# Reciprocal norms moved from GpSimd's power to ScalarE's logarithm and exponential with a Newton step on VectorE

## The reference

```python
def l2norm(t):
    return t / jnp.maximum(jnp.linalg.norm(t, axis=-1, keepdims=True), 1e-12)

def attn_layer(x, Wqkv, qs, ksc, Wo):       # HEADS = 16, DIM_HEAD = 64, windows of 32
    q, k, v = jnp.split(x @ Wqkv, 3, -1)    # then split into heads
    q = l2norm(q) * qs
    k = l2norm(k) * ksc
    q = q * cos * scale + rotate_half(q) * sin * scale
    k = k * cos * inv + rotate_half(k) * sin * inv
    out = local_attention(q, k, v)          # scores * 8, mask, softmax, times v
    return out @ Wo

for i in range(DEPTH):                      # DEPTH = 6
    x = attn_layer(shift_tokens(x), ...) + x
    x = ffn_layer(shift_tokens(x), ...) + x # layer norm, W1, a * gelu(gate), W2
```

## Time and profile before

| | |
|---|---|
| median of 3 runs | 1827.65 us (1826.91 to 1828.55) |
| the profiled execution, its own time | 1827.32 us |
| its span, first to last instruction | 1825.5 us |
| busy in the span: PE, DVE, ACT, POOL | 1684.5, 1678.9, 1451.8, 1528.1 us |
| mean granted clock of TensorE | 0.981 of full speed |

### The profile page before, as it was taken

How to read it: one execution, slowest core, us unless ns; L and a number is a source line. 1 busy time by engine, 2 the same in 40 slices (tenths; PEclk the granted TensorE clock), 3 DMA queues, 4 the chain that set the end, 5 groups by cost and what they waited for, 6 DMA issues and landing times.

```text
span 1825.5 us, 58977 instructions
## 1 busy us (share of the span) xinstructions
PE 1684.5 (92%) x19888; PEld 1377.7 (75%) x19888; DVE 1678.9 (92%) x3652; ACT 1451.8 (80%) x2786; POOL 1528.1 (84%) x1079
## 2 busy tenths in 40 slices
PE   5789999899999899999999999989999989999995
PEld 4567778777777777787777778777787877787773
DVE  6699999999999999999999999999999999999982
ACT  2568888788888788888888888878888888888872
POOL 3498988898898889889888988988898889889970
PEclk9799999999999999999999999999999999999997
DMA  5010110011201101300110201011201100100110
GB/s 143 35 42 22 28 27 25 20 29 35 82 20 28 32 20 29 97 20 20 29 32 20 90 27 28 20 29 31 86 20 29 32 20 27 28 26 20 29 34 24
DMA packets 29942, 65.49 MB, mean 36 GB/s; under 512 B 4948, under 2 KB 16216, under 8 KB 29144
## 3 DMA queue, kind: packets, MB, share of 16 engines
q1 hardware_dynamic: 29912, 65.09, 12.4%
HBM read 19.99 MB, written 1.05 MB: 12 GB/s over the span
## 4 chain that ended last, share of the span: by engine, by line
PE 33%; ACT 28%; DVE 20%; issue 15%; ACTq 2%; DVEq 2%; SPq 0%; DMA 0%; POOL 0%; POOLq 0%
PE bank L1024 25%; ACT qz L584 4%; PE bank L1149 4%; ACT sq L562 4%; ACT pz L600 4%; ACT L592 3%; ACT L621 3%; DVE n L837 3%; DVE t L832 2%; PE bank L1180 2%; DVE s L871 2%; DVE es L866 2%; DVE rot L853 2%; ACT es L592 2%; DVE t L835 2%
## 5 line engine op out<-in xcount | busy, mean ns | idle before, releaser
L395 POOL TENSOR_TENSOR rot<-t 128x512 f32<-128x512 f32 x384 | 490.9, 1289 | 137.9 <-DVE t L835 137.9
L405 POOL TENSOR_TENSOR rnorm<-n2c,minus_half 128x16 f32<-128x16 f32 x192 | 576.3, 3001 | 15.3 <-DVE n2c L846 1.0
L1024 PE MATMUL bank<-w_hi,x_hi 128*128 128x512 f32 x576 | 284.3, 494 | 8.7 <-DVE t L835 5.6
L832 DVE TENSOR_TENSOR t<-bank,rtab 128x512 f32<-128x512 f32 x384 | 260.9, 679 | 29.7 <-ACT sq L562 19.6
L418 POOL TENSOR_TENSOR es<-es,r 128x512 f32<-128x512 f32 x192 | 206.2, 1074 | 92.8 <-DVE r L876 92.8
L837 DVE TENSOR_REDUCE n<-sq 128x8 f32<-128x512 f32 x384 | 259.6, 676 | 0.0
L600 ACT ACTIVATE pz<-bank 64x512 f32<-64x512 f32 x384 | 226.1, 589 | 41.7 <-PE bank L1180 35.9
L1149 PE MATMUL bank<-ident,rot 128*128 128x128 f32 x1536 | 238.1, 278 | 17.1 <-ACT qz L584 6.7
L1024 PEld LDWEIGHTS bank<-kt,qz 128*64 128x64 f32 x6144 | 203.8, 137 | 48.0 <-issue 48.0
L562 ACT ACTIVATE sq<-bank 128x512 f32<-128x512 f32 x384 | 224.5, 595 | 17.9 <-PE bank L1024 14.5
L584 ACT ACTIVATE qz<-bank 64x512 f32<-64x512 f32 x384 | 226.0, 589 | 10.2 <-PE bank L1149 5.5
(11 more groups left out here) (102 smaller groups left out, 3464.1 us busy)
## 6 DMA issues: line engine op xcount, KB each, us to landing
vb<-v SPq DMA_DIRECT2D x96, 384.0 KB, 3.4
w_new<-in_Wqkv SPq DMA_DIRECT2D x6, 1536.0 KB, 8.7
vb<-v SPq DMA_DIRECT2D x48, 128.0 KB, 2.3
w_o<-in_Wo SPq DMA_DIRECT2D x6, 512.0 KB
w<-in_W SPq DMA_DIRECT2D x6, 341.0 KB
b<-in_b SPq DMA_DIRECT2D x6, 341.0 KB
out<-acc SPq DMA_DIRECT2D x1, 1024.0 KB, 5.1
w<-in_W SPq DMA_DIRECT2D x12, 64.0 KB
```

The costliest lines, as they stand in the source:

```text
L395: g.tensor_tensor(rot[:, i * CH:(i + 1) * CH], t1[:, b:b + CH], t2[:, b:b + CH], ALU.add)\
L405: g.tensor_tensor(rnorm[:, w], n2c[:, w], minus_half[:, :], ALU.pow).then_inc(s_rn, 1)
L832: d.tensor_tensor(heads(t1[:, b:b + CH]), src, table(n, kind, T), ALU.mult).then_inc(s_t1, 1)
L1024: return t.matmul(o, l, r, start=start, stop=stop, skip_group_check=True)
```

## The change

GpSimd's `norms` goes. In its place ScalarE computes the logarithm of `n2c` and the exponential of minus one half of it (`roots`, first approximation `first_r`), and VectorE improves that by one Newton step in three small operations (`square_root`: the square of `first_r`, that times `n2c` times -0.5, and 1.5 more times `first_r`), which writes `rnorm`. `scale_k` goes from VectorE, and GpSimd's `scale` does all four chunks. Four `roots` and four `square_root` stand in each iteration, one for each group of norms.

```diff
--- before.py
+++ after.py
@@ gpsimd
-            def norms(n, T, k):
-                w = slice((2 * T + k) * HEADS, (2 * T + k + 1) * HEADS)
-                pool.wait_ge(s_n2c, nth(4, n, 2 * T + k + 1))
-                g.tensor_tensor(rnorm[:, w], n2c[:, w], minus_half[:, :], ALU.pow).then_inc(s_rn, 1)
-            def scale_q(n, T, m):
+            def scale(n, T, m):
                 pool.wait_ge(s_add, nth(8, n, 4 * T + m + 1))
-                pool.wait_ge(s_rn, nth(4, n, 2 * T + 1))
+                pool.wait_ge(s_rn, nth(4, n, 2 * T + m // 2 + 1))
...
             def iteration(n):
-                    scale_q(n, 0, 1)
+                    scale(n, 0, 1)
+                    scale(n, 0, 2)
                     divide(m, 2)
                     rstd_(m - 1)
+                    scale(n, 0, 3)
                     add(n, 1, 0)
                     add(n, 1, 1)
-                    norms(n, 1, 0)
                     divide(m, 3)
                     add(n, 1, 2)
-                    scale_q(n, 1, 0)
+                    scale(n, 1, 0)
                     add(n, 1, 3)
-                    scale_q(n, 1, 1)
-                    norms(n, 1, 1)
+                    scale(n, 1, 1)
                     add(nx, 0, 0)
+                    scale(n, 1, 2)
                     add(nx, 0, 1)
-                    norms(nx, 0, 0)
+                    scale(n, 1, 3)
                     divide(n, 0)
-                    scale_q(nx, 0, 0)
+                    scale(nx, 0, 0)
                     divide(n, 1)
                     add(nx, 0, 2)
                     add(nx, 0, 3)
-                    norms(nx, 0, 1)
@@ scalar
+            def roots(n, T, k):
+                c = 2 * T + k
+                w = slice(c * HEADS, (c + 1) * HEADS)
+                act.wait_ge(s_n2c, nth(4, n, c + 1))
+                a.activation(logs[:, w], n2c[:, w], ACT.Ln).then_inc(s_log, 1)
+                act.wait_ge(s_log, nth(4, n, c + 1))
+                act.wait_ge(s_rn, nth(4, n - 1, c + 1))
+                a.activation(first_r[:, w], logs[:, w], ACT.Exp, scale=-0.5).then_inc(s_r0, 1)
...
                     copy_v(n, 0, 1)
+                    roots(n, 1, 0)
                     take_p(m, 2)
...
                     copy_v(n, 1, 1)
+                    roots(n, 1, 1)
                     gelu(m - 1)
...
                     exps(n, 1)
+                    roots(nx, 0, 0)
                     square(nx, 0, 2)
...
                     square(nx, 1, 0)
+                    roots(nx, 0, 1)
                     take_qk(nx, 0, 0)
@@ vector
-            def scale_k(n, T, m):
-                dve.wait_ge(s_add, nth(8, n, 4 * T + m + 1))
-                dve.wait_ge(s_rn, nth(4, n, 2 * T + 2))
-                c = heads(rot[:, (4 * T + m) * CH:(4 * T + m + 1) * CH])
-                r = rnorm[:, T * 2 * HEADS + m * CHH:T * 2 * HEADS + (m + 1) * CHH]
-                d.tensor_tensor(c, c, over(r, CHH, DH), ALU.mult).then_inc(s_ksc, 1)
+            def square_root(n, T, k):
+                c = 2 * T + k
+                w = slice(c * HEADS, (c + 1) * HEADS)
+                z, h = newton[:, 0:HEADS], newton[:, HEADS:2 * HEADS]
+                dve.wait_ge(s_r0, nth(4, n, c + 1))
+                dve.wait_ge(s_half, nth(4, n, c))
+                d.tensor_tensor(z, first_r[:, w], first_r[:, w], ALU.mult).then_inc(s_r0sq, 1)
+                dve.wait_ge(s_r0sq, nth(4, n, c + 1))
+                dve.wait_ge(s_rn, nth(4, n, c))
+                d.scalar_tensor_tensor(out=h, in0=n2c[:, w], scalar=-0.5, in1=z, op0=ALU.mult, op1=ALU.mult)\
+                 .then_inc(s_half, 1)
+                dve.wait_ge(s_half, nth(4, n, c + 1))
+                dve.wait_ge(s_sc, nth(8, n - 1, 2 * c + 2))
+                d.scalar_tensor_tensor(out=rnorm[:, w], in0=h, scalar=1.5, in1=first_r[:, w], op0=ALU.add,
+                                       op1=ALU.mult).then_inc(s_rn, 1)
...
             def iteration(n):
-                    scale_k(n, 0, 2)
+                    square_root(n, 0, 1)
                     less_max(m, 3)
...
                     guard(n, 1, 0)
-                    scale_k(n, 0, 3)
...
                     rotate(n, 1, 2)
+                    square_root(n, 1, 0)
                     split_lo(nx, (0, 1))
                     rotate(n, 1, 3)
...
                     less_max(n, 0)
+                    square_root(n, 1, 1)
                     gated(m - 1)
...
                     less_max(n, 1)
-                    scale_k(n, 1, 2)
                     sums(n, 0)
                     reciprocals(n, 0)
-                    scale_k(n, 1, 3)
...
                     middle(m, 1)
+                    square_root(nx, 0, 0)
                     rotate(nx, 0, 2)
@@ tensor
             def turn_qk(n, T, g):
-                if g < 2:
-                    pe.wait_ge(s_qsc, nth(4, n, 2 * T + g + 1))
-                else:
-                    pe.wait_ge(s_ksc, nth(4, n, 2 * T + g - 1))
+                pe.wait_ge(s_sc, nth(8, n, 4 * T + g + 1))
```

More of the change, by code:

```diff
@@ L111, in program @@
         rnorm = sb("rnorm", TILES * 2 * HEADS)
+        logs = sb("logs", TILES * 2 * HEADS)
+        first_r = sb("first_r", TILES * 2 * HEADS)
+        newton = sb("newton", 2 * HEADS)
         minus_half = sb("minus_half", HEADS)
@@ L190, in program @@
         s_rn = sem("s_rn")
-        s_qsc = sem("s_qsc")
-        s_ksc = sem("s_ksc")
+        s_log = sem("s_log")
+        s_r0 = sem("s_r0")
+        s_r0sq = sem("s_r0sq")
+        s_half = sem("s_half")
+        s_sc = sem("s_sc")
         s_qt = sem("s_qt")
@@ L396, in add @@
                  .then_inc(s_add, 1)
-            def norms(n, T, k):
-                w = slice((2 * T + k) * HEADS, (2 * T + k + 1) * HEADS)
-                pool.wait_ge(s_n2c, nth(4, n, 2 * T + k + 1))
-                if k:
-                    pool.wait_ge(s_ksc, nth(4, n - 1, 2 * T + 2))
-                g.tensor_tensor(rnorm[:, w], n2c[:, w], minus_half[:, :], ALU.pow).then_inc(s_rn, 1)
-            def scale_q(n, T, m):
+            def scale(n, T, m):
                 pool.wait_ge(s_add, nth(8, n, 4 * T + m + 1))
-                pool.wait_ge(s_rn, nth(4, n, 2 * T + 1))
+                pool.wait_ge(s_rn, nth(4, n, 2 * T + m // 2 + 1))
                 c = heads(rot[:, (4 * T + m) * CH:(4 * T + m + 1) * CH])
                 r = rnorm[:, T * 2 * HEADS + m * CHH:T * 2 * HEADS + (m + 1) * CHH]
-                g.tensor_tensor(c, c, over(r, CHH, DH), ALU.mult).then_inc(s_qsc, 1)
+                g.tensor_tensor(c, c, over(r, CHH, DH), ALU.mult).then_inc(s_sc, 1)
             def divide(n, u):
@@ L443, in iteration @@
                     add(n, 1, 2)
-                    scale_q(n, 1, 0)
+                    scale(n, 1, 0)
                     add(n, 1, 3)
-                    scale_q(n, 1, 1)
-                    norms(n, 1, 1)
+                    scale(n, 1, 1)
                 if live(nx):
                     add(nx, 0, 0)
+                if live(n):
+                    scale(n, 1, 2)
+                if live(nx):
                     add(nx, 0, 1)
-                    norms(nx, 0, 0)
                 if live(n):
+                    scale(n, 1, 3)
                     divide(n, 0)
                 if live(nx):
-                    scale_q(nx, 0, 0)
+                    scale(nx, 0, 0)
                 if live(n):
@@ L844, in guard @@
                 dve.wait_ge(s_n2, nth(8, n, 2 * c + 2))
-                dve.wait_ge(s_rn, nth(4, n - 1, c + 1))
+                dve.wait_ge(s_half, nth(4, n - 1, c + 1))
                 d.tensor_scalar(n2c[:, w], n2[:, w], 1e-24, None, ALU.max).then_inc(s_n2c, 1)
-            def scale_k(n, T, m):
-                dve.wait_ge(s_add, nth(8, n, 4 * T + m + 1))
-                dve.wait_ge(s_rn, nth(4, n, 2 * T + 2))
-                c = heads(rot[:, (4 * T + m) * CH:(4 * T + m + 1) * CH])
-                r = rnorm[:, T * 2 * HEADS + m * CHH:T * 2 * HEADS + (m + 1) * CHH]
-                d.tensor_tensor(c, c, over(r, CHH, DH), ALU.mult).then_inc(s_ksc, 1)
+            def square_root(n, T, k):
[13 more added lines that the diff above has]
+                                       op1=ALU.mult).then_inc(s_rn, 1)
             def eight(t, u):
```

## The result

| | before | after |
|---|---|---|
| median | 1828.10 us (1826.91 to 1828.87, 4 runs) | 2508.33 us (2505.01 to 2521.19, 4 runs) |
| profiled execution: own time, span | 1827.32, 1825.5 us | 2505.01, 2503.2 us |
| mean granted clock of TensorE | 0.981 | 0.899 |

The changed kernel takes 1.3735 times as long [1.3686, 1.3784]. The direction was forecast; the time lies 241 us above the forecast of 2267 and 108 us above the end of the range.

A forecast was written before the change was run, and what follows sets the result against it. No engine alone bounds; the chain runs through TensorE, ScalarE, VectorE. ScalarE's queue grows from 30.0 to 42.0 us, with waits 44.5, 9.5 more; 45 x 9.5 = 428, plus 12 lead-in, gives 2267 us, range 2160 to 2400.

The forecast's parts named there:

- the small activations: ScalarE's 8 added logarithms and exponentials of 16 columns an iteration: 0.2 us each, 1.6 us in all.
- the bare queue: ScalarE's iteration without waits, 30.0 + 12.0 = 42.0 us; as rival, only this counts: about 2145 us, chance 0.10.
- One `square_root`: Three dependent VectorE operations: 0.65 us alone, 1.35 if one meets a GpSimd add, expected only in group (1, 0).
- TensorE falls to its lower clock: Rival: ScalarE's stops gather TensorE's idle time, clock falls once an iteration, 2.5 us more: 2380 us, chance 0.12.
- lead-in: Two iterations ahead of the first Gelu, with `roots` but no feed-forward part: between 0 and 19 us, 12 taken.
- signs named beforehand as "wrong": Fewer loads, a load under 1.28 us, steady clock well under 1.00, or VectorE idle under 5 us an iteration.
- those named as "right": 478 loads, ScalarE busy over 90%, iteration 44 to 45 us, VectorE's and GpSimd's longest waits for ScalarE.
- two waits for the transposed k: ScalarE's waits of 1.8 us an iteration, expected to go because a group of `roots` stands close ahead.
- The logarithm of group (0, 1): New ScalarE wait for `n2c`, behind two `rotate`s with its `square_root` ahead of both: 0.3 us allowed.
- Group (1, 1): New wait of ScalarE's logarithm for `n2c`, a `square_root` standing between the two `rotate`s: 0.6 us.
- the small operations meet GpSimd each time: Rival: each `square_root` takes 4.5 us, VectorE becomes the bound at 48.3 us: about 2500 us, chance 0.05.
- the added loads cost nothing: Rival: one table serves logarithm and exponential, iteration follows VectorE to 34.4 us: 1800 us, chance 0.03.

The follow-up runs named there:

- e_loads: The kernel before with only the eight table loads an iteration added, two at each place of `roots`: 2260.00 us, ratio 1.2388.
- e_oneset: The changed kernel with one named table set serving both logarithm and exponential, 2 loads an iteration: 2087.99 us, ratio 1.1440.
- e_fill2: The changed kernel with 26 extra multiplications an iteration, results never read, in TensorE's three longest waits: 2374.44 us, ratio 1.2991.
- e_late: e_oneset with `roots(nx, 0, 1)` behind `take_p(n, 1)` and `guard(n, 1, 1)` right behind `rotate(n, 1, 3)`: 2041.75 us, ratio 1.1175.

## Why the prediction was wrong in size

*Right, by the runs.* The number of loads (478), their length (1.283 us each), the small activations (0.216 us for 0.2), and so the bare queue: 41.97 us for 42.0. The loads do the most damage (e_loads, +434 us; e_oneset, 420 us less without them). One `square_root`, from its first start to its last end, measured 0.68, 0.71, 1.39 and 0.68 us where the prediction had 0.65, 0.65, 1.35 and 0.65. The long one is where it was expected, as VectorE's and GpSimd's timelines show:

```profile
979.90 0.88 DVE L868 TENSOR_TENSOR newton<-first_r 128x16 f32<-128x16 f32 x1
980.82 0.17 DVE L871 SCALAR_TENSOR_TENSOR newton<-n2c,newton 128x16 f32<-128x16 f32 x1
```

```profile
979.47 1.27 POOL L401 TENSOR_TENSOR rot<-t 128x512 f32<-128x512 f32 x1 [2.49 <-DVE t L848]
```

The add ends at 980.74 and the operation that takes 0.17 alone ends at 980.78. VectorE is busy for 33.7 us of the iteration (33.6 forecast), GpSimd for 23.1 (23.6).

*The step that failed* is that the clock stayed out of the sum. "TensorE falls to its lower clock" stood among the rivals with a chance of 0.12 and 2.5 us an iteration. It was not an alternative to the forecast but a term of it: 33.7 us of work in a longer iteration, with ScalarE's stops for a group in between, means idle stretches, and the earlier trace rows already showed what can follow one. The price itself was nearly right, 2.5 us for 2.9. The working:

| term | forecast | measured | us over the run |
|---|---|---|---|
| iteration at full clock | 44.5 | 46.50 | 2.0 x 45 = 90 |
| clock, with the weight iterations | 0 | 2.9 an iteration | 2.9 x 45 = 131 |
| lead-in | 12 | 29.4 | 17 |

The second row is what the mean grew by, 49.99 - 35.59 = 14.40, less what the iteration at full clock grew by, 46.50 - 35.01 = 11.49. e_fill2, which only fills TensorE's idle time, took 2.6 of these 2.9 us off the mean and 134 us off the time. The three rows come to 238 of the 241 us; the rest is that the profiled execution is 3 us under the median. One of the signs named beforehand as "wrong" stands in the profile, a clock well under 1.00. Three of those named as "right" don't: the iteration isn't 44 to 45 us long, ScalarE is busy for 88% of the one at full clock (41.06 of 46.50) instead of over 90%, and GpSimd's longest waits are for VectorE (627.8 and 593.6 us in all), not for ScalarE.

The lead-in was mis-counted. The first Gelu starts at 188.86 us, before at 159.4. Ahead of it stand 12 of the 192 logarithms, three iterations' worth, where the prediction had two iterations. The 29.4 us are 9.8 for each of the three. That is less than the 14.4 of a full iteration, so there was some room on ScalarE, but too little to make 12 of it.

*Waits mis-sized.* Of the 2.0 us, the "two waits for the transposed k" that should go are 1.1: one of them stayed with 1.13 us. No `roots` stands between the last copy of q and that copy of k, so nothing of the change makes ScalarE late there; the prediction took it that one did. The logarithm of group (0, 1) waited 0.84 us instead of 0.3. Its clamp met GpSimd's adds, as VectorE's and GpSimd's timelines show:

```profile
961.19 1.20 DVE L859 TENSOR_SCALAR n2c<-n 128x16 f32<-128x16 f32 x1
...
985.20 0.17 DVE L859 TENSOR_SCALAR n2c<-n 128x16 f32<-128x16 f32 x1
```

```profile
959.83 2.52 POOL L401 TENSOR_TENSOR rot<-t 128x512 f32<-128x512 f32 x2
```

The adds end at 962.35, this clamp at 962.39; the one at 985.20 meets no add and takes 0.17 us. It is the collision of the earlier trace rows, which the prediction priced for `square_root` and not for the clamp ahead of a logarithm. Group (1, 1) waited 0.80 us for 0.6: in the earlier trace rows VectorE's `rotate` starts 0.82 us behind the start of the square (758.66 - 757.84) and not 0.60, which makes the forecast 0.85. A 0.30 us wait at `qz` stands for the one at `pz` that was to go. As forecast, the wait for `less_max` is gone, and those of `take_in` and `take_o` are 0.82 and 0.64 us for 1.0 and 0.6.

*The other rivals.* The bare queue needs all waits gone; 4.53 us are there. That the small operations meet GpSimd each time is out by the four lengths above. That the added loads cost nothing is refuted by e_loads. But its premise, one table for both functions, holds, and e_oneset shows what it is worth: 420 of the 680 us. The rest of that case's sum (1800 us) was wrong, since it left ScalarE's new waits out: with the loads gone the kernel still takes 2088 us. The Trainium skill ("ScalarE: Activation LUTs", Table sets) counts a single load for logarithm and exponential together; the runs agree only where the common table is named in the code, and without that the program had two a group.

*What stays open.* Of the 260 us that e_oneset loses to the kernel before, the logarithms' waits (202 us over the run) are shown as rows, but no run takes them away alone; e_late replaced them in part by others. Why one idle stretch of TensorE is followed by a fall of the clock and the next isn't, and why the iterations of e_loads are no longer at the lower clock, no run shows. A reciprocal root without any function of ScalarE or GpSimd was not tried. No version of the changed kernel beat the kernel before, and no reordering of the kernel before did either.

## What to carry to other kernels

Count the table loads in the compiled order and multiply by the load's row before anything else: on an engine with 5 us of room in 35, two functions in alternation eight times an iteration can't be hidden, and one named table for both took 420 of the 680 us back. When a change makes the iteration longer, ask in which stretches TensorE will stand, and put the clock into the sum as a term with a range from nothing upwards, not as a rival. A step that moves from an engine which nobody waits for into the middle of a queue which everybody waits for brings its waits with it, even if its own work is small: with the loads gone, 202 us of waits here.

## What the runs showed of the hardware

- 26 useless multiplications an iteration, put where TensorE stood, made the kernel faster by 134 us (2508 to 2374), with the granted clock up from 0.899 to 0.968 and no change in the iteration at full clock; 24 at twelve places, most of them on the path, raised the clock to 0.940 and won nothing.
- A fall of the clock to 0.50 (1.2 GHz) stood behind stretches of 2.5 us with TensorE busy for 0.13 and 0.65 us, in a kernel whose TensorE is busy for 75% of the span; another such stretch, with 0.67 us busy, was followed by none.
- In the changed kernel the same iteration took 46.50 us at a granted clock of 1.00 and 50.88 us at 0.87; in the kernel before with only the loads added it took 44.66 us at 0.96 and 44.14 us at 0.92.
- A table load takes 1283 ns wherever it stands, and where the function behind it waits for nothing, it starts 1.29 us after the load's start (952.83 to 954.12 in the iteration at full clock).
- A product of 128x16 elements on VectorE takes 0.17 us when GpSimd is idle and took 0.88 us beside a GpSimd add of 512 columns; a clamp of that size took 0.17 and, beside such adds, 1.20 us. Both long ones ended 0.04 us behind GpSimd's instruction.
